# Second attention: value matmuls for two chunks at a time in every other step, with eight probability buffers for six

## The reference

```python
def _L1_attn_ref(x, wq, w_down, wk_up, wv_up, wo):
    H = 16; D = E // H                      # 16 heads of 8
    ...
    q = _apply_rope(q, cos, sin)
    k = _apply_rope(k, cos, sin)
    scale = 1.0 / jnp.sqrt(jnp.asarray(D, x.dtype))
    scores = jnp.einsum('bqhd,bkhd->bhqk', q, k) * scale
    pages = jnp.arange(T) // PAGE_SIZE      # pages of 32 tokens
    allowed = pages[None, :] <= pages[:, None]
    scores = jnp.where(allowed[None, None], scores, jnp.finfo(scores.dtype).min)
    attn = jax.nn.softmax(scores, axis=-1)
    out = jnp.einsum('bhqk,bkhd->bqhd', attn, v).reshape(B, T, E)
    return out @ wo
```

## Time and profile before

| | us |
|---|---|
| median of 3 runs | 2049.58 (2048.07 to 2059.95) |
| the profiled execution | 2057.51, its span 2055.8 |
| PE busy | 1768.8 (86%) |
| DVE busy | 1380.7 (67%) |
| ACT busy | 1215.2 (59%) |
| POOL busy | 503.9 (25%) |

### The profile page before, as it was taken

The page is one execution under the profiler, slowest core; times in us unless marked ns, Lnnn a source line. Parts: engine busy times, 40 slices in busy tenths (PEclk is TensorE's granted clock), DMA queues, the critical chain, the costliest instruction groups (busy, mean ns, idle before and its releaser), DMA issues. The chain is left out here.

```text
span 2055.8 us, 40806 instructions
## 1 busy us (share of the span) xinstructions
PE 1768.8 (86%) x12164; PEld 1044.6 (51%) x12164; DVE 1380.7 (67%) x2900; ACT 1215.2 (59%) x1718; POOL 503.9 (25%) x819
## 2 busy tenths in 40 slices
PE   5999999999999999942957599999989996768992
PEld 3555555555555555532853233333333335437992
DVE  6677777677767777653557688788878843445665
ACT  6888888888888888710655245566656672213441
POOL 0211111111111111124442111212212122452441
PEclk9999999999999999965988589999999995889996
DMA  4110011111111111031232513222232303111224
GB/s 173 60 34 30 29 36 36 36 36 36 36 36 34 34 36 33 15 113 44 60 90 109 170 33 55 41 47 50 37 57 37 50 2 116 35 49 50 60 60 138
DMA packets 101133, 114.79 MB, mean 56 GB/s; under 512 B 15467, under 2 KB 75212, under 8 KB 100397
## 3 DMA queue, kind: packets, MB, share of 16 engines
q1 hardware_dynamic: 90294, 98.12, 18.0%
q0 software_dynamic: 6592, 13.56, 2.0%
q10 hardware_dynamic: 4160, 2.10, 0.3%
HBM read 78.86 MB, written 34.41 MB: 55 GB/s over the span
## 5 line engine op out<-in xcount | busy, mean ns | idle before, releaser
L1167 ACT ACTIVATE a_p<-a_score 128x1024 f32<-128x1024 f32 (+3 forms) x384 | 300.8, 810 | 220.6 <-PE a_score L1184 216.8
L1272 DVE TENSOR_REDUCE a_mx<-a_misc 128x1 f32<-128x512 f32 (+3 forms) x768 | 376.1, 549 | 61.7 <-PE a_misc L1215 37.1
L288 ACT ACTIVATE a_p<-a_score 128x1024 f32<-128x1024 f32 (+3 forms) x384 | 293.3, 810 | 29.6 <-PE a_score L320 27.2
L1212 PE MATMUL a_misc<-a_k,a_q 72*128 72x512 bf16 (+3 forms) x768 | 251.9, 349 | 49.3 <-DVE a_out L1349 21.0
L233 POOL TENSOR_SCALAR_AFFINE_SELECT a_p<-a_p 128x256 f32<-128x256 f32 x256 | 124.1, 515 | 680.0 <-ACT a_p L301 680.0
L339 PE MATMUL a_out<-a_p,a_v 128*64 128x512 f32 (+3 forms) x1536 | 289.9, 499 | 0.0
L320 PE MATMUL a_score<-a_q,a_k 64*128 64x512 f32 (+3 forms) x2304 | 270.4, 362 | 9.4 <-ACT a_p L288 4.6
L301 ACT ACTIVATE a_p<-a_p 128x2560 f32<-128x2560 f32 (+1 forms) x128 | 273.1, 2134 | 1.0
L320 PEld LDWEIGHTS a_score<-a_q,a_k 64*128 64x128 f32 x2304 | 186.4, 186 | 99.3 <-issue 39.7
L1184 PE MATMUL a_score<-a_q,a_k 128*128 128x512 bf16 (+3 forms) x768 | 232.4, 329 | 1.9 <-ACT a_p L1167 1.6
L482 DVE TENSOR_TENSOR a_part<-a_part,a_p 128x1024 f32<-128x1024 f32 (+3 forms) x256 | 224.1, 875 | 7.8 <-ACT a_p L301 1.2
(11 more groups left out here) (212 smaller groups left out, 2681.7 us busy)
## 6 DMA issues: line engine op xcount, KB each, us to landing
a_xt<-xt SPq DMA_DIRECT2D x31, 512.0 KB, 3.3
a_q<-qk_parts SPq DMA_DIRECT2D x144, 64.0 KB
a_k<-qk_parts SPq DMA_DIRECT2D x144, 64.0 KB
e_xs<-f_x_rows SPq DMA_DIRECT2D x110, 64.5 KB, 1.8
qk_parts<-p_part SPq DMA_DIRECT2D x24, 256.0 KB, 2.3
xt<-a_p SPq DMA_DIRECT2D x9, 512.0 KB, 3.6
a_w<-in_l_attn_w SPq DMA_DIRECT2D x32, 128.0 KB, 2.2
values<-p_values SPq DMA_DIRECT2D x4, 1024.0 KB, 4.7
```

Source lines behind the costliest of these rows:

```text
L288: nc.scalar.activation(chunk_of(prob[p], c), score_ps[:, c % 2, :, 0:width], ACT.Tanh, scale=scale / clamp).then_inc(tanh_done, 1)
L1167: nc.scalar.activation(prob[s % RING][:, :, 0:width], score_ps[:, s % 2, :, 0:width], ACT.Exp, scale=scale).then_inc(exp_done, 1)
L1212: mm = nc.tensor.matmul(misc[:, bank, 0:keys], q_st[bn][0:ROWS, h, t * P:(t + 1) * P], k_st[bn][0:ROWS, h, key0:key0 + keys], start=True, ...
L1272: nc.vector.tensor_reduce(m[c][:, h, t:t + 1], misc[:, bank, 0:keys], AX_X, ALU.max).then_inc(free, 1)
```

## The change

`pe_step` issues value groups in every fourth slot (2, 6, 10, 14, 18, 22) and then two of them: in slot `s` those of chunks `s/2 - 3` and `s/2 - 2`. The later chunk of each pair stays in its slot, the earlier one moves back by two slots. The ring of probability buffers grows from six to eight, so ACT waits for the chunk four back instead of three.

```diff
     SLOTS = 2 * NCH
-    RING = 6
+    RING = 8
     PV_LAG = 2
...
-                if s % 2 == 0:
-                    i = s // 2 - PV_LAG
-                    m, c, bm = (u, i, b3) if i >= 0 else (u - 1, NCH + i, (b3 - 1) % BUFS)
-                    if exists(m):
-                        pe_pv(pe, m, bm, c)
+                if s % 4 == 2:
+                    for i in (s // 2 - PV_LAG - 1, s // 2 - PV_LAG):
+                        m, c, bm = (u, i, b3) if i >= 0 else (u - 1, NCH + i, (b3 - 1) % BUFS)
+                        if exists(m):
+                            pe_pv(pe, m, bm, c)
```

## The result

| us | before | after |
|---|---|---|
| median | 2052.29 (2048.07 to 2059.95, 4 runs) | 2078.26 (2074.67 to 2079.92, 4 runs) |
| span of the profiled execution | 2055.8 | 2077.1 |
| second attention in it | 538.95 | 564.11 |

The changed kernel takes 1.012 times as long, 95% interval 1.0084 to 1.0155: 26 us more by the medians, where 12 were forecast, and above the range, which ended at 2073 (the forecast started from 2049.58; with a fourth run the kernel before stands 2.7 higher). In the profiled pair the stage grew by 25.2 us and the whole span by 21.3, so all of the loss lies in the stage.

A forecast was written before the change was run, and what follows sets the result against it. PE was taken as the bound, with DVE only 4 us of slack behind. Units +11.6 us (14.5 x 0.8), load stalls -2.2 and last unit +3 gave +12: median 2061.5, span near 2068, range 2040 to 2073.

The forecast's parts named there:

- The ledger: Roll of one undisturbed unit from slot 15: PE's work falls by 1.2 us, waits grow from some 1.8 to 3.8.
- The price of a change of mode: Value groups: each change to 16-column tiles and back costs 0.21 us; a pair saves 0.20, 96 pairs 19.2 us.
- Rival 3: Clearly slower, chance 0.15: first half, drain inside a pair, 2079; second half, doubled turn_out gap plus three clock falls, 2075.
- Where PE would wait: New PE waits: 0.84 us in slot 17, 0.44 in slot 21, smaller ones for DVE in slots 0 to 14.
- The unit: One unit of the second attention takes 31.7 us instead of 30.75 and 30.96: +0.8 us a unit.
- the term of slot 17: PE waits 0.84 us for turn_out's bank, with DVE's gap inside turn_out taken as 0.52 us.
- The loop's turns: Turns between rounds of three units: no term in the sum, so 0 us.
- The last unit: Without maximum work, ACT runs dry about 1.2 us after two to three wide pairs: +3 us.
- Stalls on loads: PE's 7.5 us of stalls on operand loads, in six places, shrink by 0.36 each: -2.2 us.
- rival 1: Drain saving of 19.2 us comes back whole, 2034; holds if new waits total under 0.2 us a unit; chance 0.12.
- The ring: Probability buffers: with eight, the wait is already met, cost 0; with six, it would stop ACT.
- Rival 2: Break-even: waits of 0.84 and 0.44 are covered, about -4 us, or +3 with one of them; 2045 to 2053; chance 0.17.

The follow-up runs named there:

- narrow pairs: Kernel before with only chunks (2, 3) and (10, 11) paired and eight buffers: 2057.51, ratio 1.0017; with the loop also written out, waits kept: 2044.44, ratio 0.9924.
- e6_pairs_unrolled: Changed kernel with the loop over units 1 to 12 written out, its slot 0 waiting until every shared bank is free: ratio 1.0089 to the kernel before.
- light engines: Changed kernel with half of each DVE reduce and half of each ACT exponential left out: 2061.72; kernel before with the same cuts: 2048.98.

## Why the prediction was right or wrong

Two steps failed. The ledger let PE's waits grow by 2.0 us a unit and they grew by 2.4 to 2.5; and it had no term for the turns of the loop, which cost 5.6 us more. Units (+4.5 over the forecast), turns (+5.6), the last unit (+2.0) and the load stalls (+0.6) make 12.7 of the 13 us that the stage grew beyond the forecast. That the change costs through waits of PE was right.

**The price of a change of mode: right.** 96 groups of 16 records, entered in 0.095; a pair of 512 takes 1.84 to 1.85 us from start to next (forecast 1.86), 512 + 384 takes 1.63, 256 + 128 0.78. The starts show it alone; the 0.42 of the narrow pairs in the loop is the same size, but their written-out unit shows that DVE can take it back. Rival 3's first half, a drain inside the pair, fell.

**Where PE would wait: right.** The ledger put waits of 0.84 in slot 17, 0.44 in slot 21 and of 0.05 to 0.37 in slots 3 to 14. Measured: 0.78 to 1.13, 0.46, and from slot 3 on 0.12, 0.20, 0.18, 0.07, 0.36, 0.31, 0.05, 0.24, 0.05, 0.11, 0.26, 0.10, 0.15, 0.16, 0.16, 0.05: nearly one for one. Taking DVE's or ACT's work away removed those laid to it. DVE's idle time of 0.8 to 1.2 after a wide pair shows in its 22 us of added idle.

**The unit: +0.8 forecast, +1.15 measured.** One part is the term of slot 17. I took DVE's gap in turn_out at 0.52, from one unit. It is 0.5, 0.7 or 0.89 by which of the three units of a turn it is, so the wait is 0.96 to 1.13 in two units of three, 0.1 of it ACT's. The trace of the kernel before had told this already, in the two units ahead of the one I read (timeline of DVE, merged):

```profile
1351.24 0.79 DVE L1302 TENSOR_TENSOR heads<-a_misc,a_rs 128x32 f32 x4 [0.89 <-DVE a_rs L1296]
...
1382.01 0.80 DVE L1302 TENSOR_TENSOR heads<-a_misc,a_rs 128x32 f32 x4 [0.71 <-DVE a_rs L1296]
```

There a value group covered it; the change took the cover away. On average that is some 0.1 of the missing 0.35. The other waits of the new order sum to what the ledger had (2.6 us in slots 0 to 14). The rest lies on the side of the old order: I took its waits at 1.8 us, and counted by starts in the two units of the earlier trace rows they are 1.54 and 1.68. The like units of the changed kernel (31.92 and 32.11) have 3.98 and 4.17. So the waits grew by 2.44 and 2.49 and not by 2.0, while PE's own work fell by 1.3, as forecast (1.2). In 14 units that makes 16.1 us for the 11.6 of the sum.

**The loop's turns: 0 forecast, +5.6 measured in the profiled pair.** The ledger rolled one undisturbed unit and had no term for the turn, though the earlier trace rows stood before me; the second half of rival 3 had it, as three falls of the clock from the longer waits, within a chance of 0.15 and only with a doubled gap. It happened as that rival said, three falls of 6.8 us, and the total fits it better (2075 in it, 2078 measured) than it fits the forecast. Its condition was a gap twice the 0.52; it was up to 0.89, and the gap made the mean wait of slot 17 longer by 0.1 us a unit and not by 0.5. So that its sum came so close is in part luck. I gave too small a chance to a price that was plain to read. Three falls of 6.8 us are also the high case: in the other profiles of pairs with the loop, one to three of the turns have one, mostly of 3.4 us. The timed runs put the whole part that needs the loop, slot 17's longer gap included, at some 9 to 14 us.

**The last unit: +3 forecast, +5.0 measured.** Mechanism right (half of ACT's work removes it, single groups half of it), size off: I counted two to three dry stretches of 1.2; the rows show four of 1.3 to 1.8.

**Stalls on loads: -2.2 forecast, -1.6 measured.** About right, and the experiments show why it matters: this is what rival 1 would have met. It said 3.6 would come back; with light engines the stalls were 29.5 us, 10 more than in the old order with the same engines (one run each). So rival 1's condition, waits under 0.2, would not have been enough.

**The ring: the cost 0 was right, the sentence beside it wrong.** Six buffers don't stop ACT. I had counted buffers and not the time at which each is wanted.

**Rival 2** fell: both waits came. Taking the one of slot 17 away didn't bring break-even either: with turn_out moved the ratio stayed at 1.0122, and with the gap gone the pairs are still 12 to 16 us over the old order written out the same way.

**What stays open.** Why the clock fell behind all three turns in the profile of the changed kernel and behind one of three before. In the 4 us before PE went on, PE was busy 2.27, 2.10 and 2.35 us at the three turns of the kernel before, and the clock fell at the first alone. A turn isn't needed for it: in `e6_pairs_unrolled`, which has none, the clock fell twice for 3.4 us with no idle stretch of PE over 0.7 us just before (the stretch of the first, columns as in the earlier trace rows):

```profile
1364.30:1367.70 3.40, 3.40 (x18) 1.18 (x19) 2.62 (x5) 1.92 (x3) 0.90 (x2) 0.50 0.02 5
```

With the loop written out and its waits kept, the one profile of the pairs had no fall in the stage, and that of the old order two of 3.4 us, each at a stall on loads. Open too is why the turn itself is some 0.5 us longer in the paired orders.

## What to carry over

When PE feeds two engines through a few small buffers, moving its work into fewer, longer blocks saves the changes of mode (0.21 us each here) but here starved both engines for the length of the block; compare that length with what the buffers hold, not the engines' busy shares. A ledger of one undisturbed unit must be read against more than one unit of the trace, and needs a term for what is not an undisturbed unit: loop turns, the last unit, and what a shorter unit then waits for. A saving seen in one order need not stand in another: the narrow pairs' 0.42 us fell to 0.04 once the loop was gone. Here the better edit lay beside the one tried: writing the loop out, with its waits kept, gave 0.8%.

## What the runs showed of the hardware

- The Trainium skill, TensorEngine Tiling (Array Packing), section Key Properties, says that a change of tiling mode drains TensorE. The runs agree and size it: 0.21 us for the way in and out at full clock, at every width, and nothing between two chunks of one mode (a pair of 512 takes 1.84 to 1.85 us from start to next, two single groups with their entries 2 x 1.08).
- A turn of this loop leaves PE idle for 1.8 to 2.7 us, and the granted clock stood at 1.2 GHz behind four of the six turns of the two profiles, for 6.8 us each time. It also fell for 3.4 us at one stall on loads of each (2.2 and 2.9 us), and in `e6_pairs_unrolled` without a turn or a stall of that length.
- Between turn_out's reciprocal and the products that need it DVE idles 0.5 to 0.9 us in slot 15 and 0.2 to 0.5 in slot 9 in the loop, by unit, and 0.03 us when the loop is written out; the four products take 0.79 us in the loop and 0.48 written out. In the loop their addresses are computed in registers; that this is the cause was not tried alone.
- Where PE waits for the 19 loads of a unit, it goes on 16 to 20 us after the first issue, and a unit leaves them about 17. SyncE's issues alone stretch over 8 us of it. No earlier start was tried.
